# Layer norm of the next tile split in two on VectorE, its second half moved behind the first FFN block, in an adaLN transformer layer on eight cores

## The reference

```python
mod = (_silu(c) @ wmod).reshape(32, 6, 1, -1)
sa, ca, ga, sb, cb, gb = mod parts
h = _layernorm(x) * (1 + ca) + sa
x = x + ga * attn(h)                       # causal attention, rotary q and k
h = _layernorm(x) * (1 + cb) + sb
x = x + gb * ffn(h)

def ffn(x):                                # every operand is rounded to FP4 in blocks of 16
    gate, y = fp4_linear(x, w_gate), fp4_linear(x, w_up)
    return fp4_linear(silu(gate) * y, w_down)
def fp4_linear(x, w): return fp4_quant_dequant(x) @ fp4_quant_dequant(w).T
def fp4_quant_dequant(x):                  # per block of 16 along the last dim
    scale = max(max|x| / 6, 1e-12)
    return GRID[searchsorted(MID, |x / scale|)] * sign * scale
```

## Time and profile before

| what | value |
|---|---|
| time, median of 2 runs | 11482.66 us (11481.42 to 11483.91) |
| the profiled execution's own time | 11458.17 us |
| its span, core 3, the slowest | 11456.6 us |
| spans of the eight cores | 11266.0 to 11456.6 us |
| busy share of the span: VectorE, TensorE, ScalarE | 61%, 51%, 10% |

### The profile page before, as it was taken

How to read it: one execution, slowest core, us unless ns; L and a number is a source line. 1 busy time by engine, 2 the same in 40 slices (tenths; PEclk the granted TensorE clock), 3 DMA queues, 4 the chain that set the end, 5 groups by cost and what they waited for, 6 DMA issues and landing times.

```text
span 11456.6 us, 79967 instructions; the slowest of 8 cores (11266.0 to 11456.6 us)
## 1 busy us (share of the span) xinstructions
PE 5863.1 (51%) x21080; PEld 2205.4 (19%) x21080; DVE 6958.1 (61%) x17486; ACT 1099.0 (10%) x2066; POOL 100.6 (1%) x120
## 2 busy tenths in 40 slices
PE   1000156756775678467844454545554444544545
PEld 0000022212221222122212222222221222212222
DVE  6787653235323532443257777677777777777777
ACT  0000001220121013101300000000000000000000
POOL 0000000000000000000000000000000000000000
PEclk6555567767666677677867677677776777767777
DMA  3101111011101200211020000000000000000000
GB/s 66 49 30 52 53 28 30 30 39 23 27 30 44 22 22 30 52 15 37 15 81 11 15 11 11 11 15 12 11 13 13 11 11 15 10 13 11 15 11 11
DMA packets 181183, 289.76 MB, mean 25 GB/s; under 512 B 106428, under 2 KB 118972, under 8 KB 179720
## 3 DMA queue, kind: packets, MB, share of 16 engines
q1 hardware_dynamic: 63688, 237.28, 6.2%
q0 software_dynamic: 117056, 47.36, 3.5%
HBM read 247.45 MB, written 84.51 MB: 29 GB/s over the span
## 4 chain that ended last, share of the span: by engine, by line
DVE 42%; PE 29%; DVEq 14%; issue 7%; DMA 5%; ACT 2%; POOL 1%; SPq 0%; ACTq 0%; POOLq 0%
DVEq L91 13%; PE pG L744 3%; PE pG L946 3%; PE pG L619 2%; DMA xt<-xmid_scr 2%; PE pA L696 2%; PE pA L598 2%; PE pB L598 2%; PE pEF L726 2%; PE pG L726 2%; DVE qd_g_f L441 2%; PE pC L721 2%; PE pD L721 2%; PE pH L926 2%; DVE qd_q_f L441 2%
## 5 line engine op out<-in xcount | busy, mean ns | idle before, releaser
L873 PE MATMUL pA<-wgT,xqf 128*128 128x512 bf16 x1536 | 658.9, 429 | 1289.2 <-DVE hmid L905 1081.6
L946 PE MATMUL pG<-wdT,hqf 128*128 128x512 bf16 x2816 | 1044.6, 550 | 173.1 <-DVE hqf L931 173.1
L926 PE MATMUL pH<-identb,hq_t 128*128 128x128 bf16 x1408 | 180.5, 306 | 1256.8 <-DVEq L913 1256.8
L666 DVE COPY recipb<-pG 128x512 f32<-128x512 f32 x128 | 88.5, 692 | 1077.9 <-PE pG L660 1077.9
L879 PE MATMUL pC<-wuT,xqf 128*128 128x512 bf16 x1536 | 657.1, 428 | 0.0
L717 ACT ACTIVATE union<-pA 128x512 bf16<-128x512 f32 (+1 forms) x640 | 354.9, 555 | 2826.5 <-PE pA L702 1758.8
L873 PE MATMUL pB<-wgT,xqf 128*128 128x512 bf16 (+1 forms) x1536 | 594.8, 387 | 0.0
L879 PE MATMUL pD<-wuT,xqf 128*128 128x512 bf16 (+1 forms) x1536 | 587.8, 383 | 0.0
L946 PEld LDWEIGHTS pG<-wdT,hqf 128*128 128x128 bf16 x2816 | 355.0, 131 | 809.7 <-issue 749.9
L598 PE MATMUL pA<-union,wbuf 128*128 128x512 bf16 x1024 | 335.8, 487 | 247.1 <-DVE stag L604 95.5
L744 PE MATMUL pG<-union 128*128 128x512 bf16 x1024 | 360.8, 530 | 193.4 <-DVE xw L759 161.7
(11 more groups left out here) (163 smaller groups left out, 10604.5 us busy)
## 6 DMA issues: line engine op xcount, KB each, us to landing
xt<-x SPq DMA_DIRECT2D x128, 512.0 KB, 4.0
xmid_scr<-xw SPq DMA_DIRECT2D x64, 512.0 KB, 2.9
xt<-xmid_scr SPq DMA_DIRECT2D x64, 512.0 KB, 4.0
out<-xw SPq DMA_DIRECT2D x64, 512.0 KB, 2.9
wmb<-wmod POOLq DMA_DIRECT2D x12, 1024.0 KB, 10.3
wbuf<-wq POOLq DMA_DIRECT2D x32, 256.0 KB, 7.2
wbuf<-wk POOLq DMA_DIRECT2D x32, 256.0 KB, 7.2
wbuf<-wv POOLq DMA_DIRECT2D x32, 256.0 KB, 7.5
```

The lines of the kernel that those rows point to most:

```text
L873: self.op('T', lambda E, cc=c, o=io, w=iw, p=pGt: E.matmul(p[:, 0:w], self.xqf[:, cc, :], self.wgT[:, cc, o:o + w], start=(cc == 0), stop= ...
L926: self.op('T', lambda E, cc=c, k2=kk, hq=hqt[i]: E.transpose(pH[:, k2, :], hq[:, cc * 128:(cc + 1) * 128], self.identb[:]), chT if kk == n ...
L946: st=(ib == 0 and c == 0), sp=lastd: E.matmul(pG[:, ha * 512:(ha + 1) * 512], self.hqf[:, k2, :], self.wdT[:, ig, ha * 512:(ha + 1) * 512] ...
```

## The change

Three things are changed.

1. `_emit_ln_mod` is split into `_emit_ln_stats` (statistics, `Ln`, `Exp`) and `_emit_ln_apply` (the two passes). The wait for ScalarE ahead of the first pass is dropped, the one ahead of the second stays. Both halves still stand back to back in the attention loop.
2. `stage_b` of the FFN is split into `stage_b1` (load and statistics), which stays where it was, and `stage_b2` (two passes and `_emit_qd`), which is recorded behind block 0.
3. `_emit_qd` gets an `engine_nop` behind line 423 that counts on `chV` once its input has been read, and the next `Silu` waits for that mark (`qd_srcfree`) in place of the end of `_emit_qd`.

```diff
@@ _emit_qd
                  s['xn'][:, 0:pw].rearrange("p (a b) -> p a b", b=16), src3, 1.0,
                  rs_b, ALU.mult, ALU.mult)))
         dr('V')
+        V('V', lambda E: E.engine_nop(), self.chV)
+        self.qd_srcfree = self.chV.n
         each(lambda srcp, dstp, pw, nbl, src3, rs_b, sc_b, s:
@@
-    def _emit_ln_mod(self, x_ap, out_ap):
+    def _emit_ln_stats(self, x_ap):
...
         self.op('S', lambda E: E.activation(self.rstd[:], self.lnv[:], AF.Exp, scale=-0.5), chS)
+        return chS.n
+
+    def _emit_ln_apply(self, x_ap, out_ap, smark):
+        chV, chS = self.chV, self.chS
         self.drain('V')
-        self.wait('V', self.chS)
         self.op('V', lambda E: E.scalar_tensor_tensor(
             self.tmp_t[:], x_ap, self.mv2[:, 0:1], self.CA1[:], ALU.subtract, ALU.mult))
-        self.wait('V', chS)
         self.drain('V')
+        self.wait('V', chS, smark)
         self.op('V', lambda E: E.scalar_tensor_tensor(
             out_ap, self.tmp_t[:], self.rstd[:], self.SAt[:], ALU.mult, ALU.add), chV)
         self.drain('V')
+
+    def _emit_ln_mod(self, x_ap, out_ap):
+        smark = self._emit_ln_stats(x_ap)
+        self._emit_ln_apply(x_ap, out_ap, smark)
@@ _emit_ffn
-        def stage_b(tc):
+        def stage_b1(tc):
...
-            self._emit_ln_mod(self.xt[b][:], self.h2x[:])
+            return self._emit_ln_stats(self.xt[b][:])
+
+        def stage_b2(tc, smark):
+            b = tc % 2
+            self._emit_ln_apply(self.xt[b][:], self.h2x[:], smark)
             self._emit_qd([(self.h2x[:, 0:512], self.xq_t[:, 0:512], 512),
...
-        xq_ready = stage_b(0)
+        xq_ready = stage_b2(0, stage_b1(0))
...
-            if tc + 1 < NTC:
-                xq_ready = stage_b(tc + 1)
+            b1_mark = stage_b1(tc + 1) if tc + 1 < NTC else None
...
                 qdm = emit_vblock(k, gu_mark)
-                self._qdm_prev = qdm
+                self._qdm_prev = self.qd_srcfree
                 prev = (k, qdm)
+                if k == 0 and b1_mark is not None:
+                    xq_ready = stage_b2(tc + 1, b1_mark)
```

## The result

| | before | changed |
|---|---|---|
| median | 11447.76 us (42 runs) | 11540.46 us (44 runs) |
| ratio | | 1.0089, 95% interval 1.0062 to 1.0117 |
| profiled execution, span | 11456.6 us | 11524.9 us |
| first opening copy of an FFN tile | 5877.1 us | 5790.1 us |
| first to last of the 64 opening copies | 5508.2 us | 5659.9 us (+151.7) |

The kernel became slower by 0.9%, about 100 us; forecast were +108 us (0.9%). The median of before given ahead of the prediction (11482.66) came from two runs, the one here from 42; the ratio compares runs on the same chips. The profile of the kernel before is of an execution in which some cores had a lower clock and ran longer, so the last row is checked on all eight cores further down.

The account below looks back on a forecast made before the run. The prediction took VectorE's order of work to bound the FFN. Its terms, 123 + 28 + 1 - 6 - 41 + 3 = +108 us, gave 11590 us, 0.9% slower, with a range of 11510 to 11670.

Parts of the forecast that it names:

- VectorE's order sets the time, and the Silu of block 0 becomes the last wait: FFN: VectorE, 75% busy, sets the time; after the move it waits from the statistics to block 0's Silu, 5.7 us.
- The new chain: Mid-sequence FFN tile, opening copy to copy of `hqf` 0: 46.1 us against 44.0; +123 us over 56 tiles with further nops.
- First tiles of a sequence: FFN: copy of `hqf` at 45.7 us against 38.7; plus 7.1 us with the nops, four times, +28 us.
- Sum in the FFN: First to last opening copy: 123 for mid-sequence tiles, 28 for first tiles, less 4 for three sequence starts, +147 us.
- The term for the norm ahead of a sequence's first tile: FFN: the first pass runs under the wait for `rstd`, saving 1.4 us four times, -6 us.
- Attention's norm loop: Attention: the first pass starts without the 0.71 us wait for `rstd`, less a 0.07 drain, 64 times, -41 us.
- The release of Silu: FFN blocks 1 and 2: Silu may start some 10 us earlier, but nothing waits for it, 0 us.
- A nop at 0.05 us: 324 nops in preparation and FFN, each taken at 0.05 us; rival of 0.3 us each gives 11670 us, chance 0.05.
- The table load: Rival: ahead of block 0's Silu a further 1.4 us wait shows on the chain, 84 us, 11675 us; chance 0.03.
- The clock rivals: FFN TensorE clock: warmer, about 11360 us, chance 0.08; colder, block 0's matmuls slower, about 11990 us, chance 0.05.
- the lower bound: FFN: full clock in every block 0, Silu ends at 10.5 us, 1.3 x 60 = 78 us less, 11512 us.

Follow-up runs that it names:

- release_only: Kernel before plus only the nop behind the last reading of the rounding's input and the earlier release of Silu; ratio 1.0050 to the kernel before.
- move_only: Changed kernel without its new nops, the earlier Silu release and attention's new `rstd` wait, leaving `stage_b2` moved behind block 0; ratio 1.0192 to the kernel before.
- after_half_gu0: Changed kernel with half of block 0's matmuls left out in each FFN tile; ratio 1.0034 to the kernel before.
- after_early_load: Changed kernel with `xt` and `xw` of the FFN as four ring buffers, so the load is issued a tile earlier; ratio 1.0105 to the kernel before.
- the early load's version: Kernel before with the norm's new order and four FFN ring buffers, the load issued a tile earlier, `stage_b` whole; ratio 0.9697 to the kernel before.
- before_half_gu0: Kernel before with half of block 0's matmuls left out in each FFN tile; ratio 0.9987 to the kernel before.
- norm_only: Kernel before with the norm's first pass no longer waiting for `rstd`, `stage_b` whole in its place; ratio 0.9885 to the kernel before.

## Why the prediction was right, and where it wasn't

- **VectorE's order sets the time, and the Silu of block 0 becomes the last wait.** Right. A wait in 64 of 64 tiles, 5.9 us each; the two pairs of experiments show that the same edit counts in one order and not in the other: half of block 0's matmuls is worth 64 us changed and 18 before (means over the cores), the early load some 9 changed and some 230 before. But it isn't TensorE alone that sets that Silu: in 22 of 56 mid-sequence tiles the chain from the load of `xt` over the statistics and ScalarE ends last.
- **The new chain, 46.1 us to the copy of `hqf` 0 against 44.0.** Measured 46.1 as a mean over the 56 tiles in mid-sequence; the other cores of the same profile show 46.0 to 46.4, so the agreement to the tenth is partly luck. The Silu ends at 11.7 (11.8 forecast), product to copy takes 34.2 (34.1). A tile takes 88.8 us, +2.2 as forecast.
- **First tiles of a sequence, +7.1.** The first of all went from 81.0 to 88.5 us, the next from 82.1 to 89.6: +7.5.
- **Sum in the FFN.** Forecast between first and last opening copy: 123 + 28 - 4 (three sequence starts) = +147 us. Measured +151.7. The term for the norm ahead of a sequence's first tile has the right size, 1.2 us each from the statistics on where 1.4 were forecast, but the loads ahead of two of them came some 1 us later, and little of it is seen in the distance.
- **Attention's norm loop, -41 us.** The four loops show -9.2 us each for 15 steps, 0.61 us a step, which is -39 for 64. The cores agree: those whose clock was never at 0.81 ahead of the FFN reach it at 5709 us before and at 5673 in the changed kernel, on average, -36 where some 38 were forecast for attention and preparation together.
- **The release of Silu, 0.** Right, by release_only and by the "issue" rows of move_only.
- **A nop at 0.05 us, taken from a difference of two gaps.** Measured 0.03 to 0.04; the sum's 16 us for them are some 12.
- **The table load.** In the changed kernel the second Silu ends 2.38 us after its load starts, as in the earlier trace rows. The further 1.38 us of the Trainium skill (ScalarE: Activation LUTs, What ACT_TABLE_LOAD costs) doesn't show, though the load now lies on the chain.
- **The clock rivals.** Neither came. The last down matmuls held VectorE for 5.2 us a tile before and after. This is right by the trace of these two kernels; no run tested it alone. The rule that the prediction takes from the Trainium skill (TensorE: Matmul & The Clock Gate, HAM oscillation), that bursts parted by waits start throttled, holds for one of the two bursts of the earlier trace rows and not for the other. Both start behind the same wait of 3.41 us for `xqf`. The one at 9467 began at 0.50, which is 1.2 GHz, and rose later; the one at 9638 was at 1.00, 2.4 GHz, from its start:

```profile
9467.40:9469.00 1.60, 1.60 (x5) 0.51 (x4) 0.00 (x0) 0.00 (x0) 0.00 (x0) 0.50 1.00 294
9638.80:9640.00 1.20, 1.20 (x7) 0.53 (x6) 0.00 (x0) 0.00 (x0) 0.00 (x0) 1.00 1.09 331
```

- **Wrong: the lower bound.** The prediction priced full clock in every block 0 at 1.3 us a tile, as if only matmuls stood between the opening copy and the Silu. after_half_gu0 shows that a second chain, load, statistics, `Ln`, `Exp` and table load, ends at 11.0 us on average. The bound should have been 0.7 us a tile, 42 us. The range was a little too wide below for that reason; the forecast didn't rest on it. The expectation of after_early_load missed too: 0.5 us less for a tile was expected and 0.1 was seen, there because the wait for the down matmuls grew.
- **The profiles' difference, 68 us, is not the ratio's 100.** Ahead of the FFN the changed kernel's profile gained 87 us where the edit is worth some 38. The last section says what differs. The measured parts, +152 in the FFN and -36 ahead of it, give +116, inside the ratio's interval (71 to 134 us). The forecast's +108 lies between the ratio's 100 and this sum; neither is sharp enough to tell them apart.

## What to carry to other kernels

Before work is moved away from a place, ask what it covers there: a serial engine's block that seems to delay the next one may be what hides another engine's matmuls. Add up the new chain from a fixed point to the next one, with the wait that now ends last, and don't count the waits that vanish; here two waits shrank and the tile grew. Ask also what the new last wait depends on: here it brought TensorE's clock into the time of a tile, which before had not mattered. Cover is to be found where the busy engine truly idles (here at the last down matmuls): the norm moved there whole, with the rounding left where it was, won 2.5% on top of the early load's version.

## What the runs showed of the hardware

The part ahead of the FFN varied between executions far more than its edits are worth, with the granted TensorE clock. From 1350 to 5650 us, columns as in the earlier trace rows, of the kernel before and of before_half_gu0, which has the same instructions there:

```profile
1350.00:5650.00 4300.00, 2877.43 (x9196) 923.36 (x9196) 1668.41 (x1543) 669.46 (x1346) 87.58 (x100) 0.70 0.14 31
```
```profile
1350.00:5650.00 4300.00, 2797.62 (x9486) 918.68 (x9487) 1694.95 (x1562) 710.41 (x1421) 89.74 (x104) 0.76 0.15 31
```

At a clock of 0.70 the FFN's first opening copy came at 5877 us, at 0.76 at 5765. In norm_only, whose attention is that of the changed kernel, it came at 5900 with 0.68, in the changed kernel at 5790 with 0.73.

Beneath these means lies a third value of the granted clock beside 0.50 and 1.00. A stretch of attention in the kernel before:

```profile
2885.00:2970.00 85.00, 63.05 (x232) 24.02 (x233) 18.26 (x15) 0.00 (x0) 0.00 (x0) 0.81 0.00 0
```

On that core the clock was at 0.81 for 1685 us ahead of the FFN, and never in it; its first opening copy came at 5877 us. Two other cores of the same execution had none ahead of the FFN and reached it at 5700 and 5718. Over all cores of the eleven profiles, those with no such time came to the FFN at 5657 to 5758 us, those with more than 1200 us of it at 5836 to 5900. Cores 0 and 1, 2 and 3, 4 and 5, 6 and 7 had it for about the same time in every profile. What brings it on, no run tested.

In the FFN of the kernel before, bound by VectorE, it does no harm (5491.5 to 5511.0 us from first to last opening copy with 0 to 2350 us of it). In the changed kernel, where block 0's matmuls are no longer hidden, the two cores with some 680 us of it took 5672.5 and 5678.1 us, the six without any 5653.7 to 5659.9. So a few tenths of a per cent were read from that stage's rows and not from the medians.
